# New step orders for all engines in a two-layer graph kernel, with four batches written out at the end

## What is computed

```python
h = relu(layernorm(x))                                   # per batch: 256 x 384
q, k, v = heads(h @ Wq + bq), heads(h @ Wk + bk), heads(h @ Wv + bv)      # 6 heads of 64
x = x + merge(softmax(q @ k.T / 8 + (0 where adj else -9e15)) @ v) @ Wf + bf
h = relu(layernorm(x))
g = h @ W                                                # 12 heads of 32
attn = leaky_relu(tanh(g) @ w_src + (tanh(g) @ w_dst).T, 0.2)
o = elu(softmax(attn where adj else -999) @ g + b)
gate = sigmoid(h @ H_w.T + H_b)
x = x + gate * o + (1 - gate) * h
```

## Time and profile before

| | us |
|---|---|
| median of 3 runs (1311.97 to 1313.68) | 1312.39 |
| the profiled execution | 1314.09 |
| its span | 1312.0 |

### The profile page before, as it was taken

One profiled execution on the slowest core, in us unless ns is written; L12 is line 12 of the kernel. 1 busy time (PEld: TensorE's weight loads), 2 busy tenths in 40 slices (PEclk: granted clock), 3 DMA queues, 4 the chain that ended last, 5 costly groups with the idle time before them and its releaser, 6 DMA issues.

```text
span 1312.0 us, 33368 instructions
## 1 busy us (share of the span) xinstructions
PE 1268.4 (97%) x10511; PEld 919.0 (70%) x10511; DVE 1208.4 (92%) x4399; ACT 1251.8 (95%) x3699; POOL 914.8 (70%) x1104
## 2 busy tenths in 40 slices
PE   5999999999999999999999999999999999999974
PEld 3667677777777677777777777777777767777642
DVE  5789999999999999999999999999999999999986
ACT  5699999999999999999999999999999999999986
POOL 5664776767776776776676777676777677677752
PEclk9999999999999999999999999999999999999987
DMA  5000000000000000000000000000000000000000
GB/s 175 13 1 16 27 15 28 25 16 27 28 16 28 25 16 28 27 28 15 27 14 27 28 27 15 28 26 15 27 28 15 27 25 16 28 27 16 13 13 24
DMA packets 29838, 33.74 MB, mean 26 GB/s; under 512 B 10465, under 2 KB 29665, under 8 KB 29665
## 3 DMA queue, kind: packets, MB, share of 16 engines
q1 hardware_dynamic: 29664, 31.62, 7.7%
HBM read 19.03 MB, written 12.58 MB: 24 GB/s over the span
## 4 chain that ended last, share of the span: by engine, by line
PE 88%; DVE 4%; ACT 3%; POOL 2%; issue 1%; DMA 1%; SPq 1%; POOLq 0%; DVEq 0%; ACTq 0%
PE job L616 27%; PE pt L689 18%; PE job L628 14%; PE unit L663 7%; PE job L711 7%; PE job L757 6%; PE job L604 4%; PE unit L680 3%; PE job L766 2%; DMA xb<-in_x_dram 1%; ACT p L867 1%; PE job L612 1%; DVE unit L1103 1%; POOL prod L1254 1%; DVE y L1109 1%
## 5 line engine op out<-in xcount | busy, mean ns | idle before, releaser
L867 ACT ACTIVATE p<-y,min 128x256 f32<-128x256 f32 x768 | 394.4, 539 | 0.9 <-DVE min L1109 0.8
L1103 DVE SCALAR_TENSOR_TENSOR unit<-unit,s,dst 128x256 f32<-128x256 f32 x768 | 335.8, 482 | 15.8 <-ACT dst L855 2.5
L689 PE MATMUL pt<-ident,p 128*128 128x128 f32 x2304 | 331.9, 276 | 11.7 <-ACT p L867 6.5
L616 PE MATMUL job<-w,h 128*128 128x384 f16 x1728 | 313.0, 327 | 1.8 <-DVE h L1008 1.7
L689 PEld LDWEIGHTS pt<-ident,p 128*128 128x128 f32 x2304 | 268.3, 142 | 42.6 <-ACT p L867 13.2
L1109 DVE CUSTOM_DVE_ANT_0 y<-unit,mask 128x256 f32<-128x256 f32 x768 | 290.4, 414 | 0.0
L1232 POOL TENSOR_SCALAR p<-p,rec 128x256 f32<-128x256 f32 x384 | 179.6, 486 | 121.2 <-DVE rec L1042 120.8
L616 PEld LDWEIGHTS job<-w,h 128*128 128x128 f16 x1728 | 169.3, 98 | 98.6 <-DVE h L1008 2.5
L877 ACT ACTIVATE pT<-pt 128x512 f32<-128x512 f32 x384 | 233.0, 625 | 1.8 <-PE pt L689 1.8
L628 PE MATMUL job<-h,w 128*128 128x256 f16 x1728 | 216.2, 274 | 2.3 <-DVE h L1008 2.1
L823 ACT ACTIVATE p<-y,min 128x256 f32<-128x256 f32 x384 | 191.1, 504 | 13.8 <-PE pt L689 7.9
(11 more groups left out here) (115 smaller groups left out, 2297.0 us busy)
## 6 DMA issues: line engine op xcount, KB each, us to landing
xb<-in_x_dram SPq DMA_DIRECT2D x32, 384.0 KB, 3.2
out_dram<-y SPq DMA_DIRECT2D x32, 384.0 KB, 2.5
pT<-in_w_all_dram SPq DMA_DIRECT2D x4, 576.0 KB, 7.6
adj_raw<-in_adj_dram SPq DMA_DIRECT2D x32, 64.0 KB, 1.8
prod<-in_w_all_dram SPq DMA_DIRECT2D x1, 576.0 KB, 5.3
p<-in_w_all_dram SPq DMA_DIRECT2D x1, 576.0 KB, 6.1
out_row<-in_bf_dram SPq DMA_DIRECT2D x1, 192.0 KB, 6.1
src_row<-in_w_src_dram SPq DMA_DIRECT2D x1, 192.0 KB, 6.8
```

Of the source, the lines that this page charges most:

```text
L616: last = mm(bank[:, 0:H], rows[:, i, c, t * P:(t + 1) * P], w16[:, w, j, c, :], start=n == 0, stop=(c, i, j) == (NC - 1, *TERMS[-1]))
L689: last = nc.tensor.transpose(pt_ps[u % 2][:, (2 * hh + kt) * P:(2 * hh + kt + 1) * P], probs[:, u % 3, hh, kt * P:(kt + 1) * P], ident[:])
L867: last = op(p1[:, u % 3, hh, :], y1[:, u % YB, hh, :], ACT.Exp, bias=min1[:, u, hh:hh + 1], scale=-1.0, accum_out=sum1[:, t, h:h + 1])
L1103: V.scalar_tensor_tensor(leaky[:, hh * T:(hh + 1) * T], bank[:, hh * T:(hh + 1) * T], s8[par][:, t, h:h + 1], dst5[:, c % 2, hh, :], ALU.a ...
```

## The change

All five lists of all five engines are written anew: STARTING, ORDERS and ENDING. ENDING covers batches 28 to 31 in full where it covered the last two, so the loop has 25 passes, n = 3 to 27. Steps, instructions, banks and buffers are the same; which job gets which of the three banks follows from the new order. One wait is added: for batches 1 to 3 `aggregate` also waits for the RSTD step of the batch before. The long lists are cut to their first lines (STARTING), to GpSimd's and the last of VectorE's (ENDING); ORDERS is whole.

```diff
 STARTING = {
     "PE": steps("""
-        SUMS_T 0 0, SPREAD 0 0, BIAS_V 0 0, LN_T0 0 0, SUMS_T 1 0, LN_T0 1 0, SPREAD 1 0, Q 0 0, K 0 0,
-        SUMS_T 2 0, Q 1 0, QK 0 0, Q 2 0, K 1 0, SPREAD 2 0, K 2 0, QK 1 0, V 0 0, V 1 0, LN_T0 0 1, PT0 0 0,
-        PT0 1 0, LN_T0 1 1, QK 2 0, Q 0 1, Q 1 1, PT0 2 0, K 0 1, PT0 3 0, K 1 1, PT0 4 0, PT0 5 0, PV0 0 0,
...
+        SUMS_T 0 0, SPREAD 0 0, LN_T0 0 0, LN_T0 1 0, Q 0 0, SUMS_T 1 0, K 0 0, SPREAD 1 0, QK 0 0, K 1 0,
+        Q 1 0, SUMS_T 2 0, K 2 0, Q 2 0, QK 1 0, SPREAD 2 0, BIAS_V 0 0, V 0 0, V 1 0, LN_T0 0 1, LN_T0 1 1,
+        PT0 0 0, PT0 1 0, QK 2 0, Q 0 1, PT0 2 0, K 0 1, Q 1 1, PT0 3 0, K 1 1, PT0 4 0, PT0 5 0, PV0 0 0,
...
     "ACT": steps("""
-        SUM_W 0 0, SUM_W 1 0, HIGH_W 0 0, SUM_W 2 0, SUM_W 3 0, HIGH_W 1 0, LN_T0 0 0, LN_T0 1 0, SUM_W 4 0,
-        SUM_W 5 0, Q 0 0, HIGH_W 2 0, Q 1 0, HIGH_W 3 0, EXP0 0 0, EXP0 1 0, Q 2 0, V 0 0, EXP0 2 0, LN_T0 0 1,
-        V 1 0, LN_T0 1 1, EXP0 3 0, PT0 0 0, EXP0 4 0, Q 0 1, PT0 1 0, EXP0 5 0, PT0 2 0, PT0 3 0, Q 1 1,
...
+        SUM_W 0 0, SUM_W 1 0, HIGH_W 0 0, HIGH_W 1 0, LN_T0 0 0, LN_T0 1 0, SUM_W 2 0, SUM_W 3 0, Q 0 0,
+        SUM_W 4 0, HIGH_W 2 0, SUM_W 5 0, EXP0 0 0, Q 1 0, EXP0 1 0, HIGH_W 3 0, EXP0 2 0, Q 2 0, V 0 0,
+        LN_T0 0 1, LN_T0 1 1, PT0 0 0, V 1 0, PT0 1 0, EXP0 3 0, EXP0 4 0, Q 0 1, EXP0 5 0, PT0 2 0, PT0 3 0,
...
     "DVE": steps("""
-        STATS0 0 0, COLUMNS 0 0, LARGEST 0 0, SCALES 0 0, LOW_W 0 0, LARGEST 1 0, LN_T0 0 0, LN_T0 1 0,
-        LOW_W 1 0, STATS0 0 1, SCALES 1 0, BIAS_ROW 0 0, K 0 0, LOW_W 2 0, SCORES0 0 0, LARGEST 2 0,
-        SCORES0 1 0, K 1 0, LOW_W 3 0, NORMP0 0 0, K 2 0, SCORES0 2 0, NORMP0 1 0, SCALES 2 0, GATE_BIAS 0 0,
-        NORMP0 2 0, SCORES0 3 0, LN_T0 0 1, LN_T0 1 1, SCORES0 4 0, SCORES0 5 0, NORMP0 3 0, NORMP0 4 0,
-        NORMP0 5 0, K 0 1, STATS0 0 2, GATE_BIAS 1 0, SCORE_ROWS 0 0, K 1 1, PV0 0 0, PV0 1 0, SCORES0 0 1,
...
+        COLUMNS 0 0, STATS0 0 0, LARGEST 0 0, SCALES 0 0, LOW_W 0 0, LN_T0 0 0, LN_T0 1 0, LOW_W 1 0,
+        STATS0 0 1, LARGEST 1 0, K 0 0, SCALES 1 0, SCORES0 0 0, SCORES0 1 0, LOW_W 2 0, K 1 0, LARGEST 2 0,
+        K 2 0, NORMP0 0 0, LOW_W 3 0, NORMP0 1 0, SCORE_ROWS 0 0, SCORES0 2 0, BIAS_ROW 0 0, NORMP0 2 0,
+        SCALES 2 0, LN_T0 0 1, LN_T0 1 1, SCORES0 3 0, SCORES0 4 0, NORMP0 3 0, SCORES0 5 0, NORMP0 4 0, K 0 1,
+        NORMP0 5 0, GATE_BIAS 0 0, LOW_W 4 0, K 1 1, PV0 0 0, PV0 1 0, SCORES0 0 1, SCORES0 1 1, OUT0 0 0,
...
 ORDERS = {
     "PE": steps("""
-        B PV1 0, P QK 0, L LN_T0 0, B PT1 9, B PT1 10, P QK 1, A GATE 1, B PT1 11, P QK 2, L LN_T0 1, P PT0 0,
-        B PV1 1, A DST_T 0, P PT0 1, P PT0 2, B OUT_T 0, A DST 0, B OUT_T 1, L Q 0, L K 0, A DST 1, P PT0 3,
-        L K 1, P PT0 4, P PT0 5, A DST 2, P PV0 0, P PV0 1, L Q 1, A PT1 0, A PT1 1, A DST 3, P OUT0 0,
-        P OUT0 1, A DST 4, A PT1 2, L V 0, A PT1 3, L V 1, A PT1 4, L Q 2, P LN_T1 0, A DST 5, P LN_T1 1,
-        A PT1 5, L K 2, A PT1 6, P HEADS 0, A PT1 7, P HEADS 1, A PT1 8, P GATE 0
+        B PT1 8, B PV1 0, P QK 0, L LN_T0 0, B PT1 9, L LN_T0 1, B PT1 10, P QK 1, A GATE 0, B PT1 11, P QK 2,
+        L Q 0, P PT0 0, P PT0 1, A DST_T 0, B PV1 1, L K 0, P PT0 2, A DST 0, A GATE 1, B OUT_T 0, A DST 1,
+        P PT0 3, B OUT_T 1, L K 1, P PT0 4, A DST 2, P PT0 5, P PV0 0, P PV0 1, L Q 1, A PT1 0, A DST 3,
+        A PT1 1, P OUT0 0, P OUT0 1, A PT1 2, L Q 2, L V 0, A PT1 3, A PT1 4, L V 1, P LN_T1 0, P LN_T1 1,
+        A DST 4, A DST 5, L K 2, A PT1 5, A PT1 6, P HEADS 0, A PT1 7, P HEADS 1
     """),
     "ACT": steps("""
-        B PT1 8, B EXP1 10, B EXP1 11, A GATE 0, L LN_T0 0, P EXP0 0, P EXP0 1, B PT1 9, B PT1 10, A GATE 1,
-        B PT1 11, P EXP0 2, L LN_T0 1, P PT0 0, P EXP0 3, P EXP0 4, A SCALED 0, P PT0 1, P EXP0 5, P PT0 2,
-        A SCALED 1, P PT0 3, L Q 0, A EXP1 0, P PT0 4, P PT0 5, A EXP1 1, P PV0 0, A SCALED 2, P PV0 1,
-        B ELU_RELU 0, A EXP1 2, A EXP1 3, L Q 1, A PT1 0, A PT1 1, A SCALED 3, B ELU_EXP 0, A EXP1 4, A PT1 2,
-        A EXP1 5, A PT1 3, A SCALED 4, L V 0, A EXP1 6, L V 1, L Q 2, P LN_T1 0, P LN_T1 1, A PT1 4, A EXP1 7,
-        A PT1 5, A SCALED 5, A PT1 6, A EXP1 8, P HEADS 0, P HEADS 1, A PT1 7, A EXP1 9
+        B EXP1 11, L LN_T0 0, P EXP0 0, P EXP0 1, B PT1 9, B PT1 10, L LN_T0 1, A GATE 0, P EXP0 2, B PT1 11,
+        L Q 0, P EXP0 3, P PT0 0, P PT0 1, P EXP0 4, A SCALED 0, P EXP0 5, P PT0 2, A GATE 1, A SCALED 1,
+        P PT0 3, A EXP1 0, P PT0 4, P PT0 5, A EXP1 1, A SCALED 2, P PV0 0, A EXP1 2, P PV0 1, B ELU_RELU 0,
+        A PT1 0, A SCALED 3, A PT1 1, A EXP1 3, B ELU_EXP 0, L Q 1, A EXP1 4, A PT1 2, L Q 2, A EXP1 5, L V 0,
+        A PT1 3, A EXP1 6, A PT1 4, L V 1, P LN_T1 0, P LN_T1 1, A SCALED 4, A EXP1 7, A PT1 5, A SCALED 5,
+        A PT1 6, A EXP1 8, A PT1 7, P HEADS 0, P HEADS 1, A EXP1 9, A PT1 8, A EXP1 10
     """),
     "DVE": steps("""
-        B SCORES1 7, L STATS0 0, C FINISH 0, A LN_T1 0, A LN_T1 1, B SCORES1 8, P K 2, B SCORES1 9, A SKIP_H 0,
-        C FINISH 1, B SCORES1 10, B SCORES1 11, B PV1 0, P SCORES0 0, P SCORES0 1, L LN_T0 0, B RECIP1 0,
-        P SCORES0 2, P NORMP0 0, P SCORES0 3, P NORMP0 1, A SCORE_SUM 0, P NORMP0 2, P SCORES0 4, B PV1 1,
-        L LN_T0 1, A DST_T 0, P SCORES0 5, P NORMP0 3, B OUT_T 0, P NORMP0 4, B OUT_T 1, A SCORES1 0,
-        P NORMP0 5, A SCORES1 1, L K 0, A SCORES1 2, L K 1, A SCORES1 3, P PV0 0, P PV0 1, A SCORES1 4,
-        A SCORES1 5, P OUT0 0, P STATS1 0, P OUT0 1, P STATS1 1, P AGGREGATE1 0, A SCORES1 6
+        L STATS0 0, B SCORES1 7, A LN_T1 0, A LN_T1 1, B SCORES1 8, A SKIP_H 0, B SCORES1 9, P K 2,
+        B SCORES1 10, B SCORES1 11, B PV1 0, P SCORES0 0, P SCORES0 1, B RECIP1 0, L LN_T0 0, P SCORES0 2,
+        P NORMP0 0, P SCORES0 3, L LN_T0 1, P NORMP0 1, A SCORE_SUM 0, C FINISH 0, P NORMP0 2, P SCORES0 4,
+        P SCORES0 5, A DST_T 0, P NORMP0 3, L K 0, C FINISH 1, P NORMP0 4, B PV1 1, A SCORES1 0, P NORMP0 5,
+        B OUT_T 0, A SCORES1 1, L K 1, B OUT_T 1, A SCORES1 2, A SCORES1 3, P PV0 0, P PV0 1, A SCORES1 4,
+        A SCORES1 5, P OUT0 0, P OUT0 1, P STATS1 0, P STATS1 1, P AGGREGATE1 0, A SCORES1 6
     """),
     "POOL": steps("""
-        L RSTD0 0, L NORM0 0, A SCORE_PROD 0, C OUT_SUM 0, P NORMP0 0, P NORMP0 1, P NORMP0 2, A MASK1 0,
-        P NORMP0 3, P NORMP0 4, P NORMP0 5, A GATES 0, B ELU_BIAS 0, L MASK0 0, P RES_ROW 0, A SKIP 0,
-        P RSTD1 0, P NORM1 0
+        L RSTD0 0, L NORM0 0, A SCORE_PROD 0, P NORMP0 0, P NORMP0 1, A MASK1 0, P NORMP0 2, P NORMP0 3,
+        P NORMP0 4, P NORMP0 5, B ELU_BIAS 0, L MASK0 0, A GATES 0, P RES_ROW 0, C OUT_SUM 0, P RSTD1 0,
+        P NORM1 0, A SKIP 0
     """),
     "SP": steps("""
-        L LOAD_X 0, C STORE 0, L LOAD_ADJ 0
+        L LOAD_X 0, L LOAD_ADJ 0, C STORE 0
     """),
 }
...
 ENDING = {
     "POOL": steps("""
-        RES_ROW 0 0, SCORE_PROD 0 1, NORMP0 0 0, OUT_SUM 0 3, NORMP0 1 0, MASK1 0 1, NORMP0 2 0, NORMP0 3 0,
-        GATES 0 1, NORMP0 4 0, NORMP0 5 0, SKIP 0 1, ELU_BIAS 0 2, RSTD1 0 0, NORM1 0 0, OUT_SUM 0 2,
-        SCORE_PROD 0 0, MASK1 0 0, GATES 0 0, SKIP 0 0, ELU_BIAS 0 1, OUT_SUM 0 1, ELU_BIAS 0 0, OUT_SUM 0 0
+        RSTD0 0 1, NORM0 0 1, SCORE_PROD 0 3, NORMP0 0 2, NORMP0 1 2, MASK1 0 3, NORMP0 2 2, NORMP0 3 2,
+        NORMP0 4 2, NORMP0 5 2, RES_ROW 0 2, OUT_SUM 0 5, ELU_BIAS 0 4, MASK0 0 1, GATES 0 3, RSTD1 0 2,
+        NORM1 0 2, SKIP 0 3, RSTD0 0 0, NORM0 0 0, SCORE_PROD 0 2, NORMP0 0 1, MASK1 0 2, NORMP0 1 1,
+        NORMP0 2 1, NORMP0 3 1, RES_ROW 0 1, NORMP0 4 1, NORMP0 5 1, OUT_SUM 0 4, MASK0 0 0, ELU_BIAS 0 3,
+        GATES 0 2, RSTD1 0 1, NORM1 0 1, SKIP 0 2, SCORE_PROD 0 1, NORMP0 0 0, NORMP0 1 0, NORMP0 2 0,
+        MASK1 0 1, NORMP0 3 0, NORMP0 4 0, NORMP0 5 0, RES_ROW 0 0, GATES 0 1, ELU_BIAS 0 2, OUT_SUM 0 3,
+        RSTD1 0 0, NORM1 0 0, SCORE_PROD 0 0, MASK1 0 0, SKIP 0 1, GATES 0 0, OUT_SUM 0 2, ELU_BIAS 0 1,
+        OUT_SUM 0 1, SKIP 0 0, ELU_BIAS 0 0, OUT_SUM 0 0
     "DVE": steps("""
...
-        SCORES1 8 1, SCORES1 9 1, SCORES1 10 1, SCORES1 11 1, SCORE_SUM 0 0, SKIP_H 0 0, DST_T 0 0, PV1 0 1,
-        RECIP1 0 1, SCORES1 0 0, SCORES1 1 0, SCORES1 2 0, SCORES1 3 0, SCORES1 4 0, SCORES1 5 0, SCORES1 6 0,
-        SCORES1 7 0, PV1 1 1, SCORES1 8 0, OUT_T 0 1, OUT_T 1 1, SCORES1 9 0, SCORES1 10 0, SCORES1 11 0,
-        PV1 0 0, FINISH 0 1, RECIP1 0 0, FINISH 1 1, PV1 1 0, OUT_T 0 0, OUT_T 1 0, FINISH 0 0, FINISH 1 0
...
+        SCORES1 7 1, FINISH 0 2, LN_T1 0 0, LN_T1 1 0, SCORES1 8 1, FINISH 1 2, SCORES1 9 1, SCORES1 10 1,
+        SCORES1 11 1, SCORE_SUM 0 0, RECIP1 0 1, DST_T 0 0, PV1 0 1, SCORES1 0 0, SCORES1 1 0, PV1 1 1,
+        SCORES1 2 0, OUT_T 0 1, SCORES1 3 0, OUT_T 1 1, SCORES1 4 0, SCORES1 5 0, SCORES1 6 0, SCORES1 7 0,
+        SCORES1 8 0, FINISH 0 1, SCORES1 9 0, FINISH 1 1, SCORES1 10 0, SCORES1 11 0, SKIP_H 0 0, PV1 0 0,
+        RECIP1 0 0, PV1 1 0, OUT_T 0 0, OUT_T 1 0, FINISH 0 0, FINISH 1 0
...
-FIRST, LAST = 3, 2
+FIRST, LAST = 3, 4
 
 
```

(2 more changed lines are left out.)

200 lines of the change are left out of this document (117 added, 83 removed).

## The result

The changed kernel takes 1350.74 us (median of 4 runs, 1348.97 to 1351.14) against 1312.38 before on the same chip: ratio 1.0286, 95% interval [1.0274, 1.0298]. The forecast was 1313.1, with a range up to 1317.5; it is 37.6 us too low. The profiled execution took 1350.66, its span 1348.6.

The account below looks back on a forecast made before the run. TensorE was taken as the bound, idle only in fill and drain. Loop +0.5, start -0.7, single-answer edits 0, drain +0.9 gave +0.7 us: 1314.8 profiled, 1313.1 as median (1.7 below); 8 in 10 range 1307 to 1317.5.

Parts of the forecast that it names:

- the term of the loop: 25 loop passes: 0.16 us lost at Q 2 against 0.10 won at PT1 6, +0.5 us, bounds -2.5 to +3.8.
- the drain: Last steps after the loop: -1.4 + 2.6 + 0.4 - 0.7 = +0.9 us, bounds -2.5 and +3.5.
- Edits with one answer: Added RSTD waits of batches 1 to 3 and LOAD_ADJ ahead of STORE on SyncE's queue: nothing, up to 0.2 us.
- the start: First steps and fill: TensorE 1.0 us later through the load of x, fill -1.7; in all -0.7 us.
- The 0.10 us before PT1 6: TensorE's one real wait in a loop pass; the new list, with K 2 ahead of PT1 5, removes its 0.10 us.
- a wait before Q 2: TensorE in the loop waits for ScalarE's copy of Q 1, with zero slack: 0.16 us lost a pass.
- the meeting of SKIP and SCORE_SUM: Drain, batch 31: GpSimd's two SKIP operations hold VectorE's SCORE_SUM, which grows by 1.4 to 3.0 us; taken as +2.6.
- SCORE_SUM of batch 30: Drain, VectorE: OUT_SUM on GpSimd no longer runs beside it, -1.4 us on the way to the last exponentials.
- a clock that drops in other places: Sign against the prediction: TensorE's clock dropping in other places of the drain than before; no size given.
- The rule of the Trainium skill: GpSimd and VectorE share an SBUF interface; two FINISH beside NORMP0 held up to 0.9 us each, sum same or up to 1 more.

Follow-up runs that it names:

- the kernel with both edits: The changed kernel with the store issued one pass later on SyncE's queue and SCORES1 7 ahead of STATS0 on VectorE; 1320.27 us, ratio 1.0057.

## Why the prediction was wrong, point by point

- **The step that failed** is the term of the loop: +0.02 us a pass, +0.5 for 25 passes, +3.8 at most. It was added up from TensorE, ScalarE and VectorE; SyncE and the DMA were in no sum, and GpSimd only in the drain, so the landing of x against STATS0 was put at nothing without a reason. The runs showed 1.1 us a pass there, +27.2 us for the loop, which is gone (passes of 38.91) as soon as the x load stands ahead of the late store or STATS0 behind SCORES1 7.
- **Where it was in reach.** The sentence under "Edits with one answer" (LOAD_ADJ ahead of STORE, "so the store, and FINISH 1 that waits for the store before, lose nothing") is true and asks the wrong question: what is moved behind LOAD_ADJ, and not what is queued behind the store, which is the x load of the next pass. I had walked GpSimd's new list for the drain, but not its new loop list, in which OUT_SUM, the store's condition, goes from behind SCORE_PROD to behind RES_ROW.
- **The same error on VectorE.** STATS0 now stands ahead of SCORES1 7. For the start I had priced exactly this kind of move (STATS0 of batch 1 waiting for x with LARGEST and K behind it), and didn't ask it of the loop, where it comes 25 times. A wait that needs two edits can't be found by pricing each alone: with the x load ahead of the late store, or with STATS0 behind, nothing is lost, as the runs show.
- **It was near a threshold.** The trace before has RES_ROW, the issue of x and the end of SCORES1 6 at

```profile
585.55 1.82 POOL L1244 TENSOR_TENSOR xc<-xb,out_row 128x768 f32<-128x768 f32 x1
...
587.47 0.37 SPq L531 DMA_DIRECT2D xb<-in_x_dram  x1
...
593.71 0.08 DVE L1109 DVE_READ_ACCUMULATOR2_ANT min<- 128x1 f32 x1
```

With OUT_SUM right behind RES_ROW that gives 587.4 + 1.8 + 0.5 + 3.5 = 593.2 against 593.8, no wait (3.5 is a landing in the company of the store; alone it is 3.2, so this trace would have left 0.9 us). The rest comes from RES_ROW being 1.7 us later against VectorE in the new list (1.7 - 0.6 = 1.1). An honest sum would have given "between 0 and some 2 us a pass, unknown", a range to 1363 (1313.1 + 25 x 2), instead of nothing.
- **The loop apart from that:** right in kind. The 0.10 us before PT1 6 is gone and a wait before Q 2 came in its place: PT1 2 to Q 2 takes 0.55 us for 0.44, so 0.11 where I said 0.16. Hand-overs elsewhere are 0.05 better, so a pass is 38.91 and not 38.98: -1.3 us for 25 passes instead of +0.5.
- **The start:** its mechanism was right. VectorE stood 1.81 us ahead of STATS0 of batch 1 (3 forecast; x landed at 19.9 and not at 20.5), HIGH_W 2 started at 23.73 (24.2 forecast, 23.10 before), TensorE came 1.6 us later to PV0 0 of batch 0 (42.2 to 43.8; 1.0 forecast) and made it good in the fill. The window from 80 to 120 is full now (40.00 for 38.25). The number is not confirmed: TensorE is 1.0 us ahead at HEADS 0 of batch 3 in this pair of executions, 0.5 without the other order (0.7 forecast), but executions with the same start differ by more. The 13 with the new start are there at 169.2 to 171.7 (mean 170.0), the four with the old one at 169.8 to 171.9 (mean 170.6), which leaves about 0.1 us. That the pair fits the forecast is luck.
- **The drain:** the meeting of SKIP and SCORE_SUM was right: SCORE_SUM of batch 31 at 4.9 us (3.4 to 5 forecast), 2.9 us of drain and 3.3 us of time by the run that moves SKIP, against +2.6. SCORE_SUM of batch 30 fell from 3.38 to 1.95, but moved by itself this brought nothing measurable at the end (-1.4 forecast). Missed were the clock (0.74 for 0.88 between HEADS and PT1 0 of batch 31, which goes with 3.4 to 3.9 us of drain in executions of one and the same list) and the passes written out, +3.2, of which FINISH beside SCORE_PROD is 2.2. The prediction had named a clock that drops in other places as a way to be wrong. Why it drops in some executions stays open.
- **The rule of the Trainium skill** that I weighed for FINISH (up to 0.9 us each) was right for GpSimd's TENSOR_TENSOR: my sum looked at NORMP0 in the loop and not at SCORE_PROD in the written-out passes. Beside GpSimd's TENSOR_SCALAR I had read only VectorE's side. In the loop of the kernel with both edits FINISH 1 and a TENSOR_SCALAR of NORMP0 start together; FINISH 1 keeps its length and the TENSOR_SCALAR, 0.48 us by itself, takes 1.25, once in nearly every pass (timelines of VectorE and GpSimd, one row each):

```profile
343.41 0.97 DVE L1183 SCALAR_TENSOR_TENSOR y<-o1m,gate 128x768 f32<-128x768 f32 x1
343.40 1.25 POOL L1274 TENSOR_SCALAR p<-p,rec 128x256 f32<-128x256 f32 x1
```

In the kernel before, FINISH 0 held a small TENSOR_SCALAR (0.19 us by itself) for 0.81 in the same way, 26 times. So the two engines do exclude each other there; GpSimd pays, and since it has the time the passes cost nothing more (38.91 and 38.96).

The Trainium skill says (DMA: Bandwidth & Descriptors, Anatomy of one DMA — SWDGE (gpsimd) path) that DMA engines don't wait on semaphores, and that any wait happens on the issuing sequencer before dispatch. It says so where it describes a DMA issued by GpSimd; the trace has the same for SyncE: the x load was issued 0.5 us after the store, though its buffer had been free for 2.3. I hadn't applied the rule.

## What to carry to other kernels

A queue that issues DMAs in order is an engine like the others: draw it into every list of edges, and for each instruction in it ask what is behind it, not only what is ahead. Where a transfer's data is needed at the start of a pass, compute landing against need (end of the releaser + issues ahead on the queue + time to land) for the new orders of all engines together, and give a threshold within half a microsecond of zero the full price in the range. When an experiment gives the expected number, look at which wait paid for it before believing the reason.

## What the runs showed of the hardware

- Two DMA issues of SyncE in a row are 0.5 us apart (602.82 and 603.33; 0.38 us busy), in some passes 0.8 (642.75 and 643.57).
- 384 KB of x land 3.1 to 3.2 us after their issue (median) when no store is issued within 1.7 us, and 3.6 when they are issued 0.5 us behind a store of 384 KB. Single loads take 4.3 to 4.9, once 6.1 us. So a slack of 0.5 us is used up in one pass of 27.
- VectorE and GpSimd exclude each other: a VectorE cast of 0.18 us took 1.66 to 1.72, a two-input operation of 0.95 us took 2.2, GpSimd's TENSOR_TENSOR of 1.82 became 2.42, and its TENSOR_SCALAR of 0.48 became 1.25.
- The same instructions in the same order drained in 75.9 or 79.8 us, with a granted clock of 0.89 or 0.74 in one stretch of it.
